# A maximum over penalised experts in place of a gated sum, in the last expert stage of a vision tower

## What is computed

```python
def _L3_ffn_ref(x, W1, b1, Wg, bg, Wd, bd):     # C = 64, HID = 256, E = 8
    xf = x.reshape(-1, orig_shape[-1])
    H = jax.nn.gelu(xf @ W1 + b1, approximate=False)
    probs = jax.nn.softmax((H @ Wg + bg) / TEMP, axis=-1)
    assign = jnp.argmax(probs, axis=-1)
    out = jnp.zeros_like(xf)
    for e in range(Wd.shape[0]):
        y = H @ Wd[e] + bd[e]
        sel = (assign == e)[:, None]
        out = out + jnp.where(sel, probs[:, e:e + 1] * y, 0.0)
    return out.reshape(orig_shape)
...
    h = _layernorm(h + _L3_ffn_ref(h, ...), axis=-1)
```

## Time and profile before

| | us |
|---|---|
| median of 3 runs | 146.95 |
| lowest and highest run | 146.9 and 147.11 |
| the profiled execution | 147.45 |
| its span | 145.7 |

### The profile page before, as it was taken

The page is one execution under the profiler, slowest core; times in us unless marked ns, Lnnn a source line. Parts: engine busy times, 40 slices in busy tenths (PEclk is TensorE's granted clock), DMA queues, the critical chain, the costliest instruction groups (busy, mean ns, idle before and its releaser), DMA issues.

```text
span 145.7 us, 2991 instructions
## 1 busy us (share of the span) xinstructions
PE 132.5 (91%) x1159; PEld 73.4 (50%) x1159; DVE 94.8 (65%) x302; ACT 65.3 (45%) x138; POOL 44.3 (30%) x99
## 2 busy tenths in 40 slices
PE   6999999999997996899989869998999999999960
PEld 2445466676963533554543324663454465554640
DVE  6506747789844386666778998639466577306991
ACT  3564970385600101791442015365850565568252
POOL 8819887578740000045000034000592000000000
PEclk9999999999999999999999999999999999999999
DMA  5999993000000000000020000000000000000001
GB/s 163 296 413 375 219 360 154 0 4 0 4 0 0 0 4 0 0 2 0 16 50 0 0 2 4 0 4 0 0 0 0 0 4 0 0 4 0 2 0 41
DMA packets 3830, 7.74 MB, mean 53 GB/s; under 512 B 1596, under 2 KB 1820, under 8 KB 3816
## 3 DMA queue, kind: packets, MB, share of 16 engines
q1 hardware_dynamic: 3504, 7.44, 15.6%
q10 hardware_dynamic: 312, 0.11, 0.3%
HBM read 7.18 MB, written 0.15 MB: 50 GB/s over the span
## 4 chain that ended last, share of the span: by engine, by line
PE 64%; DVE 24%; ACT 5%; issue 3%; POOL 3%; DVEq 0%; ACTq 0%
PE ps L472 12%; PE ps L532 5%; PE ps L519 4%; PE ps L479 4%; PE ps L487 3%; DVE scores L1536 3%; PE ps L635 3%; DVE residual L1657 3%; PE ps L526 2%; DVE patch_sb L1649 2%; PE ps L692 2%; PE ps L684 2%; PE ps L501 2%; DVE scores_rest L1557 2%; ACT hidden L1036 2%
## 5 line engine op out<-in xcount | busy, mean ns | idle before, releaser
L472 PE MATMUL ps<-idle_operand 128*128 128x512 bf16 x123 | 34.1, 393 | 3.2 <-DVE scores L1536 1.6
L1028 ACT ACT_TABLE_LOAD x16 | 20.5, 1283 | 0.3
L472 PEld LDWEIGHTS ps<-idle_operand 128*128 128x128 bf16 x123 | 10.4, 102 | 16.9 <-issue 3.2
L1016 ACT ACTIVATE squares<-ps 128x288 f32<-128x288 f32 x7 | 2.9, 412 | 30.2 <-PE ps L783 8.4
L379 POOL CAST combine_parts_T<-combine_parts_T 64x288 f32<-64x288 bf16 x2 | 0.8, 418 | 36.3 <-DVE combine_parts_T L1271 36.3
L1243 DVE COPY centred<-ps 128x288 f32<-128x288 f32 x7 | 3.2, 457 | 11.6 <-ACT squares L1016 11.6
L1323 DVE TENSOR_TENSOR hidden_gated<-hidden,ps 128x576 f32<-128x576 f32 x12 | 8.4, 751 | 3.3 <-PE ps L526 3.3
L967 PE MATMUL ps<-weights_sb,hidden 128*128 128x256 f32 (+2 forms) x28 | 9.8, 472 | 0.0
L1036 ACT ACTIVATE hidden<-ps,weights_sb 128x576 f32<-128x576 f32 x12 | 8.5, 739 | 2.4 <-PE ps L519 2.1
L1536 DVE TENSOR_REDUCE scores<-ps 128x32 f32<-128x512 f32 (+1 forms) x13 | 7.7, 655 | 0.7 <-PE ps L835 0.7
L444 POOL TENSOR_TENSOR patch_sb<-scores,top 128x288 f32<-128x288 f32 (+1 forms) x2 | 1.6, 782 | 18.2 <-DVE top L1545 18.1
(11 more groups left out here) (344 smaller groups left out, 280.7 us busy)
## 6 DMA issues: line engine op xcount, KB each, us to landing
patch_sb<-patches SPq DMA_DIRECT2D x6, 288.0 KB, 5.2
weights_sb<-weights SPq DMA_DIRECT2D x1, 717.0 KB, 14.0
weights_sb<-weights SPq DMA_DIRECT2D x1, 689.0 KB, 12.7
weights_sb<-weights SPq DMA_DIRECT2D x1, 640.0 KB, 7.0
weights_sb<-weights SPq DMA_DIRECT2D x1, 532.0 KB, 7.8
weights_sb<-weights SPq DMA_DIRECT2D x1, 512.0 KB, 10.6
weights_sb<-weights SPq DMA_DIRECT2D x1, 394.0 KB, 11.3
selectors<-sels SPq DMA_DIRECT2D x1, 384.0 KB, 10.1
```

Of the source, the lines that this page charges most:

```text
L472: mm(PS[:, bank, :], idle_in[:, 0:P], idle_in[:, :], start=True, stop=True)
L1028: act.activation(warm[:, tables[0]:tables[0] + 1], warm[:, 0:1], func)
```

## The change

For a token, every expert that was not chosen gets a penalty of -2^126 added to its outputs in PSUM, so that the maximum over the eight experts is the output of the chosen one. The pieces:

- VectorE turns `t8[2]` into `pen3` (0 for the chosen expert, -2^126 for the others, bfloat16), instead of making `comb`.
- TensorE turns `pen3` over with five transposes (one per tile) into PSUM at rows 96 to 103, ScalarE copies them in two pieces (192 and 384 columns) into rows 96 to 103 of `PEN3`, whose other rows GpSimd has filled with ones. `BD3` grows by eight rows, 96 to 103, in which GpSimd puts an identity over experts, repeated per feature.
- The `bias` matmul is gone; `choose` adds biases and penalties together in one bfloat16 matmul, at the end of a tile instead of at its start.
- TensorE's order becomes: cleared bank, `logits_T` of chunk 0, first part of tile 0, `logits_T` of chunk 1, second part of tile 0, the two logits transposes, both parts of tile 1, the first part of tile 2, the five penalty transposes, the second part of tile 2, `choose` for tiles 0, 1 and 2, and then the halves of tiles 3 and 4, each with its two parts and its `choose`.
- VectorE takes the maximum over the experts out of PSUM into `MX3` (`chosen3`) and then multiplies by the largest probability and adds the residual `RES3` in one instruction (`scalar_tensor_tensor`).
- ScalarE's residual copies go to `RES3`, and its switch to the square root's table stands behind the two new copies.
- At the start VectorE no longer fills `one3`, and SyncE's wait for the fills counts one less.

```diff
@@ -79,6 +79,7 @@
 BCOLS = _at
 SEL1, SEL2 = 2 * E * P, E * P
 SLOT_STEP = 1024
+OUT_OF_CHOICE = 2.0 ** 126
 SAT = 3.3895313892515355e38
 LIMIT_A = 2.0 ** -64
 LIMIT_B = 0.5 * (1 + 2.0 ** -20) * 2.0 ** 64 / SAT
@@ -98,7 +99,7 @@
 k_done q_done v2_done q_hi q_rest q_mid q_low q_parts k_parts k_bcast v2_ready score_mm score_red late_keys late_keys_in top_in top_out top_sum sub2 exp2_out norm2
 prob2 prob2_t prob2_copied ctx2_done ctx2_ready
 x3_done x3_ready s3_done h3_t h3_copied exp3_in exp3_out p3_ready p3_t p3_copied0 p3_copied1
-h3_ready y3_done comb3_done wd_c logits3_T logits3_in bias3 bias3_c bias3_split hres hres_in tile3 ss
+h3_ready y3_done pen3_ones pen3_ready pen3_t pen3_in wd_c logits3_T logits3_in bias3 bias3_c bias3_split hres hres_in tile3 ss
 out_act out_dve stored""".split()
 
 
@@ -221,9 +222,12 @@
         HH = HR[:, 0:2, :, :].rearrange("p c h n -> p c (h n)")
         BR = sb("bias3_rows", [65, E * D])
         BT3, BR3 = sb("bias3_bf", [65, E * D], BF16), KF[0:65, 0:E * D]
-        BD3 = sb("bias3_parts", [65, E * D], BF16)
-        one3 = sb("ones_bf", [65, P], BF16)
-        YM = X[:, :, :].rearrange("p k t -> p (k t)")[:, 0:FT * (E + 1) * D].rearrange("p (i d e) -> p i d e", e=E + 1, d=D)
+        OUT_AT = 96
+        BD3 = sb("bias3_parts", [OUT_AT + E, E * D], BF16)
+        x_tiles = X[:, :, :].rearrange("p k t -> p (k t)")
+        RES3, MX3 = (x_tiles[:, i * FT * D:(i + 1) * FT * D].rearrange("p (q d) -> p q d", d=D) for i in range(2))
+        PEN3 = x_tiles[0:OUT_AT + E, 2 * FT * D:2 * FT * D + HALF].bitcast(BF16)
+        pen3 = sb("out_of_choice", [P, FT, E], BF16)
 
         def pieces3(q):
             return ((0, D // 2), (D // 2, D)) if q >= FT - 2 else ((0, D),)
@@ -257,6 +261,7 @@
         psBC2 = PS[:, G, 0:HALF]
         psL = PS[0:TT, MB, 0:2 * NT * E].rearrange("p (i e) -> p i e", e=E)
         psN = PS[0:TT, MB, 64:64 + 2 * NT * E].rearrange("p (i e) -> p i e", e=E)
+        psPen = PS[OUT_AT:OUT_AT + E, MB, 0:HALF].bitcast(BF16)
         psCT = PS[0:8 * E, MB, 128:128 + HALF // 2].bitcast(BF16)
 
         def cols(t):
@@ -329,7 +334,7 @@
             load("f0b", "w_f0b")
             load("r1", "w_r1")
             sp.dma_start(KB[112:120, :], maskk).then_inc(S["maskk"], 16)
-            sp.wait_ge(S["zero3"], 3)
+            sp.wait_ge(S["zero3"], 2)
             sp.dma_start(BR[0:65:32, :], bias3).then_inc(S["bias3"], 16)
             for g in ("r2", "r3"):
                 load(g, "w_" + g)
@@ -453,6 +458,10 @@
                                    d20[1][:, a * HEADS:b * HEADS].unsqueeze(2).to_broadcast([P, (b - a) * HEADS, keys]),
                                    ALU.mult).then_inc(S["norm2"], 1)
             gates32(2)
+            pool.memset(PEN3[:, :], 1.0).then_inc(S["pen3_ones"], 1)
+            pool.wait_ge(S["pen3_ones"], 1)
+            link(pool.tensor_copy(BD3[OUT_AT:OUT_AT + E, :].rearrange("p (d e) -> p d e", e=E),
+                                  c("ident", E, OUT_AT)[:, OUT_AT:OUT_AT + E].unsqueeze(1).to_broadcast([E, D, E])))
             pool.wait_ge(S["bias3_c"], 1)
             link(pool.tensor_copy(BD3[0:1, :], BR[0:1, :]))
             for r in (32, 64):
@@ -960,12 +969,14 @@
             pe.wait_ge(S["bias3_split"], 1)
             wd = w("Wd").rearrange("p (c f) -> p c f", c=2)
 
-            def bias(q, a=0, b=D):
-                mm(y3(q, a, b), one3[:, 0:n3(q)], BD3[:, a * E:b * E], start=True, stop=False, skip_group_check=True)
-
             def part(q, ch, a=0, b=D):
-                return mm(y3(q, a, b), tok3(q, ch), wd[:, ch, a * E:b * E], start=False, stop=(ch == 1),
-                          skip_group_check=True)
+                mm(y3(q, a, b), tok3(q, ch), wd[:, ch, a * E:b * E], start=(ch == 0), stop=False, skip_group_check=True)
+
+            def choose(q, a=0, b=D):
+
+                at = slice(0, 64) if q == 0 else slice(64 + (q - 1) * P, 64 + q * P)
+                mm(y3(q, a, b), PEN3[:, at], BD3[:, a * E:b * E], start=False, stop=True, skip_group_check=True)\
+                    .then_inc(S["y3_done"], 1)
 
             def logits_T(ch):
 
@@ -975,27 +986,41 @@
                 return mm(PS[0:E, MB, P:P + 64], w("Wg")[:, ch * E:(ch + 1) * E], tok3(0, ch),
                           start=False, stop=(ch == 1), skip_group_check=True)
 
-            bias(0)
             mm(PS[:, MB, 0:P + 64], idle_in[:, 0:P], idle_in[:, 0:P + 64], start=True, stop=False, skip_group_check=True)
             pe.wait_ge(S["h3_ready"], 2)
             logits_T(0)
+            pe.wait_ge(S["wd_c"], 2)
+            part(0, 0)
             pe.wait_ge(S["h3_ready"], 4)
             logits_T(1).then_inc(S["logits3_T"], 1)
-            pe.wait_ge(S["wd_c"], 2)
-            part(0, 0)
+            part(0, 1)
             pe.wait_ge(S["logits3_in"], 1)
             mm(PS[:, G + 1, E:FT * E].rearrange("p (g e) -> p g e", e=E), LT[:, 0:P],
                c("ident").rearrange("p (g r) -> p g r", r=32)[:, :, 0:E], start=True, stop=True)
             mm(PS[0:64, G + 1, 0:E], LT[:, P:P + 64], c("ident")[:, 0:E], start=True, stop=True)\
                 .then_inc(S["logits"], 1)
-            part(0, 1).then_inc(S["y3_done"], 1)
+            for ch in range(2):
+                part(1, ch)
+            part(2, 0)
+            pe.wait_ge(S["pen3_ready"], 1)
+            pe.transpose(psPen[:, 0:64], pen3[0:64, 0, :], cb("ident", 64)[:, 0:64])
             for q in range(1, FT):
+                last = pe.transpose(psPen[:, 64 + (q - 1) * P:64 + q * P], pen3[:, q, :], cb("ident"))
+            last.then_inc(S["pen3_t"], 1)
+            part(2, 1)
+            pe.wait_ge(S["pen3_ones"], 1)
+            pe.wait_ge(S["pen3_in"], 1)
+            choose(0)
+            choose(1)
+            pe.wait_ge(S["pen3_in"], 2)
+            choose(2)
+            for q in range(FT - 2, FT):
                 for a, b in pieces3(q):
                     if q == FT - 2 and a > 0:
                         pe.wait_ge(S["exp_in"], 4)
-                    bias(q, a, b)
                     part(q, 0, a, b)
-                    part(q, 1, a, b).then_inc(S["y3_done"], 1)
+                    part(q, 1, a, b)
+                    choose(q, a, b)
 
         @block.scalar
         def _(act):
@@ -1179,10 +1204,14 @@
             act.wait_ge(S["exp_in"], 4)
             act.activation(ex[:, 0:FT, :], t8[0][:, 0:FT, :], ACT.Exp).then_inc(S["exp_out"], 1)
             act.wait_ge(S["hres"], 1)
-            act.activation(YM[0:64, 0, :, E], PS[0:64, YB, 0:D], ACT.Copy).then_inc(S["hres_in"], 1)
-            act.activation(YM[:, 1:FT, :, E].rearrange("p (h b) d -> p h b d", b=2),
+            act.activation(RES3[0:64, 0, :], PS[0:64, YB, 0:D], ACT.Copy).then_inc(S["hres_in"], 1)
+            act.activation(RES3[:, 1:FT, :].rearrange("p (h b) d -> p h b d", b=2),
                            PS[:, YB, D:D + 2 * P].rearrange("p (b h d) -> p h b d", b=2, h=2), ACT.Copy)\
                .then_inc(S["hres_in"], 1)
+            act.wait_ge(S["pen3_t"], 1)
+            act.wait_ge(S["pen3_ones"], 1)
+            for a, b in ((0, 64 + P), (64 + P, TOK)):
+                act.activation(PEN3[OUT_AT:OUT_AT + E, a:b], psPen[:, a:b], ACT.Copy).then_inc(S["pen3_in"], 1)
             table(ACT.Sqrt)
 
             def squares3(q):
@@ -1329,7 +1358,6 @@
             dve.memset(CTF[:, :], 0.0).then_inc(S["rows_zero"], 1)
             dve.memset(comb3[:, :, 3 * E:4 * E], 0.0).then_inc(S["rows_zero"], 1)
             dve.memset(BD3[:, :], 0.0).then_inc(S["zero3"], 1)
-            dve.memset(one3[:, :], 1.0).then_inc(S["zero3"], 1)
             dve.memset(BR[:, :], 0.0).then_inc(S["zero3"], 1)
             dve.wait_ge(S["tok_w"], 16)
             centre_rows(OFF["tok_w"][0], P, IN_K, "rows_c")
@@ -1635,26 +1663,24 @@
             link(dve.tensor_reduce(m6[0][:, 0:FT], lg[:, 0:FT, :], AX, ALU.max))
             dve.tensor_tensor(t8[0][:, 0:FT, :], lg[:, 0:FT, :], col(m6[0], P, FT), ALU.subtract).then_inc(S["exp_in"], 1)
             top_first(t8[2], lg, m6[0], t8[1], m6[1], P, FT)
+            dve.tensor_scalar(pen3[:, :, :], t8[2][:, 0:FT, :], -1.0, OUT_OF_CHOICE, ALU.add, ALU.mult).then_inc(S["pen3_ready"], 1)
             dve.wait_ge(S["exp_out"], 4)
             link(dve.tensor_reduce(m6[2][:, 0:FT], ex[:, 0:FT, :], AX, ALU.add))
             link(dve.reciprocal(m6[3][:, 0:FT], m6[2][:, 0:FT]))
-            dve.tensor_tensor(comb[:, 0:FT, :], t8[2][:, 0:FT, :], col(m6[3], P, FT), ALU.mult).then_inc(S["comb3_done"], 1)
-            dve.wait_ge(S["comb3_done"], 1)
 
             def rows3(q):
                 return 64 if q == 0 else P
 
-            def gated3(q, a, b):
+            def chosen3(q, a, b):
                 p = rows3(q)
-                step(dve.tensor_tensor(YM[0:p, q, a:b, 0:E],
-                                       y3(q, a, b).rearrange("p (d e) -> p d e", e=E),
-                                       comb[0:p, q, :].unsqueeze(1).to_broadcast([p, b - a, E]), ALU.mult))
```

(6 more changed lines are left out.)

## The result

The changed kernel takes 149.38 us at the median of six runs, against 147.05 for the kernel before: a ratio of 1.0134 with a 95% interval of 1.0103 to 1.0166. It is slower, as forecast, but by some 2 us (1.34% of 147.05 is 1.97) where 0.5 were forecast, and outside the range. The profiled execution took 149.21 us; its span is 147.4.

The account below looks back on a forecast made before the run. The stores' issue, started by the first output after tile 3's residual, was taken to bound the kernel. VectorE starting 2.55 us later but saving 2.04 gave 0.51 later: 146.95 + 0.5 = 147.45 us, range 147.0 to 148.0.

Parts of the forecast that it names:

- T: End of tile 3's residual on VectorE; claimed to move the kernel's end one for one, from 140.46 to 140.97.
- VectorE starts later than it saves: Last stage: VectorE's first maximum comes 2.55 us later, while its cheaper tiles save 2.04 us up to T.
- The sum of TensorE's list, 7.66: TensorE's work from 129.10 until tile 0's penalty matmul is readable: 7.66 us, so first maximum at 136.79.
- My upper bound: Worst case: weight loads bare at up to three new TensorE joints, 0.57 us, plus multiply-adds' high pitch, 0.08: T +1.16.
- VectorE's 4.18: VectorE's time from the first maximum to T: three full tiles and two halves, 4.18 us instead of 6.22.
- the forecast that VectorE would not idle between tiles 0 and 4: Sign expected in the profile's last stage: no VectorE idle time between those tiles, full tiles 0.94 us apart.
- The transposes pipeline: TensorE's five penalty transposes follow at a pitch of 0.083 us, 0.42 us in all.
- the rival of 0.214 each: Five penalty transposes on TensorE each paid in full, 1.07 us instead of 0.42; time 148.1 us, chance 0.10.
- The penalty, ScalarE's copies, GpSimd and the start are covered: Penalty ready 0.69 us before TensorE needs it, copies by 0.43 and 0.23; GpSimd's additions and the start cost nothing.
- TensorE does not take over the end: Last half tile: TensorE finishes near 141.1, before VectorE reaches that half at 141.5.

Follow-up runs that it names:

- outs_first: Changed kernel with ScalarE's outputs of tiles 0 to 2 ahead of tile 3's squares, and their reciprocal earlier on VectorE; ratio 1.0122 to the kernel before.
- max_alone: Kernel before with only VectorE's maximum and multiply-add, over all eight experts without penalty, TensorE's order kept; ratio 0.9952 to the kernel before.
- early_penalty: Changed kernel with TensorE reordered: both logits chunks first, penalty transposes after tile 1's first part, tiles 0 and 1 finished before tile 2; ratio 1.0018 to the kernel before.
- small_last: Changed kernel with the penalty kept in 128 columns per tile and tile 0's 64-row transpose last of the five; ratio 1.0111 to the kernel before.
- reworked kernel: Changed kernel with early penalty order, 128-column transposes, outputs of tiles 0 to 2 first and 24 more VectorE fills; ratios 0.9975 and 0.9981 to the kernel before.
- before_plus1: Kernel before with one small fill more in VectorE's list near 6 us, where it is idle; ratio 1.0042 to the kernel before.
- shift_after: Changed kernel with 24 small fills more in VectorE's list near 6 us, where it is idle; ratio 1.0102 to the kernel before.
- wide_transposes: Changed kernel with the penalty kept in 128 columns per tile, one more GpSimd fill and one more VectorE wait; ratio 1.0102 to the kernel before.

## Why the prediction was wrong

- **T carries the end, one for one.** Right: T +1.70, end +1.70, and outs_first shows the stores' queue as the link.
- **VectorE starts later than it saves.** Right in kind, and the reason for the loss: 3.12 later (12.87 for 9.75), 1.42 saved (4.80 for 6.22). max_alone and early_penalty show both halves.
- **The sum of TensorE's list, 7.66, was mis-sized by 0.59.** This is the first step that failed. I priced each kind of work by its pitch among its own kind and put the joints at nothing "because most joints exist before as well". Enough of them did not: the six passes lost 0.19 to the joints at their two ends, the second part of tile 2 lost 0.19, the logits in two pieces 0.11, their transposes 0.08 and the penalty's 0.02; the maximum's release lost another 0.08, and TensorE began 0.05 earlier. My upper bound had 0.57 for just this, and the bound was the answer. That the two sums agree is in part luck: the bound had three bare loads of 0.19, and the rows show more joints at about 0.1 each. That a bare load is the cause was tested at the joint ahead of the transposes alone (small_last); for the others it is read from the rows.
- **VectorE's 4.18 was mis-sized by 0.62.** The second step. The maximum came as priced, 0.68 for 512 and 0.42 for 256. The multiply-add took 0.28 and 0.25 instead of 0.22 and 0.20: the row it was priced by, 0.224, multiplies by a constant, where the new one reads its factor per row from SBUF, and nothing was added for that. That this is what costs the 0.06 no run tests. With its wait this made 0.28 over the five. The other 0.34 is the stall at one place in VectorE's list, which no row of before shows, because there the instruction at that place does not wait for VectorE's own last result; I had no rival for it, and the forecast that VectorE would not idle between tiles 0 and 4 fell with it.
- **The transposes pipeline.** Right: five in 0.44 us (135.41 to 135.85) for 0.42, and the rival of 0.214 each did not come true. The 275 ns of the Trainium skill, page "TensorE: Matmul & The Clock Gate", section on PE-mode transpose, are three times the 0.088 from one to the next here, and more than the 0.19 that the record of a single one takes.
- **The penalty, ScalarE's copies, GpSimd and the start are covered.** Right: TensorE never waited for them.
- **TensorE does not take over the end.** Right for the changed kernel; VectorE reached the last half at 142.88, TensorE was done by 141.74. In the reworked kernel it does.

Added up, in the profiles' own times: T was foreseen 0.51 later; the first maximum added 0.62 (137.41 for 136.79) and VectorE 0.62, together 1.75 (142.21 for 140.46). Of this, 0.05 lies ahead of the stage and 1.70 in it.

## What to carry to other kernels

An engine's cheaper work is worth what its stage lets it start: when the saving needs one more step on the engine that feeds it, sum that engine's list up to the first use, and price every place where the loaded weights change in columns, or between 64 rows and 128. Look past the last compute instruction: a queue of stores that runs without a gap is the end, and its first entry is where to gain; that alone brought 0.35 us in the stage here, the whole rework 0.23, though their timed intervals overlap. Before crediting a change with a few tenths of a microsecond, put one idle instruction into the list and see what it moves.

## What the runs showed that I had not expected

- One harmless instruction early in VectorE's list costs 0.34 us in the stage (before_plus1), 24 of them give back 0.35 (shift_after), and so does a single wait (wide_transposes).
- A weight load runs ahead of the matmul in front of it past a type change and a satisfied wait, and past a change from 128 rows to 65 or 104, but not past a change of columns or between 128 and 64 rows: 0.43 ahead against none.
- The whole stage repeats to 0.01 us between two profiled executions, while the medians of the kernel before lay between 147.05 and 147.55: the spread comes from elsewhere; in the profiles most of it lies before the first copy, which stood between 10.48 and 11.45 us.
